# Layer 0 as 32-row products into four banks, pooling in four column groups: one change to a one-core token and attention kernel

## The reference, cut to what matters

```python
def _L0_tok_ref(x, A, W0, b0, ...):          # x: 64 x 64 frames of 75 joints and 3 channels
    x = _layer(x, A, W0, b0, g0, be0, m0, v0, relu=True)     # 3 -> 128
    x = _layer(x, A, W1, b1, g1, be1, m1, v1, relu=True)     # 128 -> 128
    x = _layer(x, A, W2, b2, g2, be2, m2, v2, relu=False)    # 128 -> 64
    return x.mean(axis=2)                                    # mean over the 75 joints
# _layer: x @ W over channels, A @ x over joints, bias, normalisation, relu
h = tok(x);  h = concat([h, txt], axis=1)                    # 64 x 96 x 64
h = h + attention(layernorm(h))
h = h + ffn(layernorm(h))                                    # 30 steps of tanh, silu, layernorm, matmul
```

## Time and profile before

| | |
|---|---|
| median of three runs | 2138.03 us |
| lowest, highest run | 2136.45, 2356.8 us |
| profiled execution, first to last instruction (span) | 2132.7 us |
| PE busy | 1903.4 us (89%) |
| DVE busy | 1674.5 us (79%) |
| ACT busy | 1153.7 us (54%) |
| `tokenise` starts / the stage after it starts | 180.8 / 1562.8 us |
| mean granted clock of TensorE | 0.977 |

### The profile page before, as it was taken

How to read it: one execution, slowest core, us unless ns; L and a number is a source line. 1 busy time by engine, 2 the same in 40 slices (tenths; PEclk the granted TensorE clock), 3 DMA queues, 4 the chain that set the end, 5 groups by cost and what they waited for, 6 DMA issues and landing times. The chain is left out here.

```text
span 2132.7 us, 61654 instructions
## 1 busy us (share of the span) xinstructions
PE 1903.4 (89%) x20166; PEld 1487.2 (70%) x20166; DVE 1674.5 (79%) x4836; ACT 1153.7 (54%) x2296; POOL 484.8 (23%) x431
## 2 busy tenths in 40 slices
PE   2316399999999999999999999999957799999998
PEld 2315277777777777777777777777747477777776
DVE  3205388888888888888888888888865788888887
ACT  0103266666666666666666666666614366666665
POOL 5000000000000000000000000000004699999997
PEclk9999699999999999999999999999987799999999
DMA  3333100000000000000000000000041100000000
GB/s 111 75 71 63 44 3 3 3 3 3 3 3 3 3 3 3 3 3 3 3 3 3 3 3 3 3 3 3 3 95 32 29 0 0 0 0 0 0 0 30
DMA packets 38153, 33.35 MB, mean 16 GB/s; under 512 B 13781, under 2 KB 35477, under 8 KB 37141
## 3 DMA queue, kind: packets, MB, share of 16 engines
q1 hardware_dynamic: 36159, 32.21, 6.4%
q10 hardware_dynamic: 1972, 0.86, 0.2%
HBM read 22.02 MB, written 11.03 MB: 15 GB/s over the span
## 5 line engine op out<-in xcount | busy, mean ns | idle before, releaser
L614 ACT ACTIVATE z1hi<-ps 128x375 f16<-128x375 f32 x820 | 398.7, 486 | 405.1 <-PE ps L556 405.1
L554 PE MATMUL ps<-AThi,y0hi 125*128 125x150 f16 x2460 | 567.1, 241 | 36.5 <-DVE z1lo L650 34.6
L555 PE MATMUL ps<-ATlo,y0hi 125*128 125x150 f16 x2460 | 584.9, 238 | 0.0
L650 DVE TENSOR_TENSOR z1lo<-ps,z1hi 128x375 f16<-128x375 f32 x820 | 445.8, 544 | 171.3 <-ACT z1hi L614 171.2
L556 PE MATMUL ps<-AThi,y0lo 125*128 125x150 f16 x2460 | 564.8, 239 | 0.0
L655 DVE TENSOR_TENSOR y<-ps,negb 125x384 f32<-125x384 f32 x820 | 451.1, 550 | 37.2 <-PE ps L571 37.2
L569 PE MATMUL ps<-W1hi,z1hi 128*128 128x128 f16 x2460 | 455.2, 219 | 0.2 <-DVE y L655 0.2
L571 PE MATMUL ps<-W1hi,z1lo 128*128 128x128 f16 x2460 | 454.1, 219 | 0.0
L570 PE MATMUL ps<-W1lo,z1hi 128*128 128x128 f16 x2460 | 453.6, 219 | 0.0
L645 DVE SCALAR_TENSOR_TENSOR y0lo<-ps,y0hi 125x512 f16<-125x512 f32 x615 | 420.7, 684 | 1.1 <-ACT y0hi L610 1.1
L610 ACT ACTIVATE y0hi<-ps 125x512 f16<-125x512 f32 x615 | 363.4, 591 | 13.4 <-PE ps L536 13.4
(11 more groups left out here) (197 smaller groups left out, 2315.4 us busy)
## 6 DMA issues: line engine op xcount, KB each, us to landing
pooled_parts<-stage SPq DMA_DIRECT2D x410, 4.0 KB
zk<-z_parts SPq DMA_DIRECT2D x16, 360.4 KB
parts<-pooled_parts SPq DMA_DIRECT2D x16, 256.0 KB, 5.7
xs<-in_x_v SPq DMA_DIRECT2D x3, 1201.2 KB
xs<-in_x_v SPq DMA_DIRECT2D x5, 720.7 KB
z_parts<-zp SPq DMA_DIRECT2D x20, 180.2 KB
pooled_parts<-stage SPq DMA_DIRECT2D x205, 2.0 KB
pooled_parts<-stage SPq DMA_DIRECT2D x205, 10.0 KB
```

What stands on the lines that cost most here:

```text
L554: nc.tensor.matmul(o, hi, ahi, start=(ph == 0), stop=False, skip_group_check=True)
L555: nc.tensor.matmul(o, hi, alo, start=False, stop=False, skip_group_check=True)
L614: nc.scalar.activation(z1hi[:, q, 0:GV], ps[:, Z1B + q % 2, 0:GV], ACT.Identity).then_inc(z1hi_done, 1)
L650: nc.vector.tensor_tensor(z1lo[:, q, 0:GV], ps[:, Z1B + q % 2, 0:GV], z1hi[:, q, 0:GV], ALU.subtract).then_inc(z1lo_done, 1)
```

## The change

Layer 0 becomes twelve products of 32 rows and 128 columns. For each piece, quarter q multiplies rows 32q to 32q + 31 of the operand with the matching rows of `W0K`, and writes to bank q (banks 0 to 3, three times 128 columns each). The operand is no longer a slice of `zk` at an address from a register, but one of two fixed buffers `z_static` (`zst`), which SP fills by a transfer (`fetch`) two iterations ahead. y0 high and low become four steps of 384 columns, one for each quarter, in place of three of 512. The twelve products stand together, after mix of quarter 1. Pooling becomes twelve float32 products of 128 columns: quarter q writes output partitions 32q to 32q + 31, the three pieces add up in PSUM, and the result lies in the last 128 columns of bank 0, beside layer 0's. `stage` is then 128 x 128, SP stores it in four transfers to one array, and the addition in `tokens` is gone.

The core of the diff:

```diff
-        y0hi = sb("y0hi", [P, 2, PH, QUART * C], F16)
-        y0lo = sb("y0lo", [P, 2, PH, QUART * C], F16)
+        ZW = GV + 3
+        zst = sb("z_static", [P, 2, ZW + 1], F16)
+        y0hi = sb("y0hi", [P, 2, QUART, PH * C], F16)
+        y0lo = sb("y0lo", [P, 2, QUART, PH * C], F16)
         z1hi = sb("z1hi", [P, QUART, PH * P], F16)
         z1lo = sb("z1lo", [P, QUART, PH * P], F16)
         y1 = sb("y1", [P, 2, QUART, PH * C])
-        stage = sb("stage", [96, 2, QUART, C])
-
+        stage = sb("stage", [P, 2, C])
...
-        STORES = [(0, 0, 2, 0), (0, 2, 1, 32 + MID), (0, 3, 2, 64 + 3), (1, 0, GF, 32)]
-        Y0B, Z1B, Y1B, PLB = 0, 3, 5, 7
+        Y0B, Z1B, Y1B = 0, 4, 6
+        PLC = PH * C
...
+        def pooled_rows(it):
+            return pooled_dram.rearrange("(q f) c -> q f c", q=QUART)[:, bass.ds(it * GF, GF)]
...
+                def fetch(it, par):
+                    sp.dma_start(zst[:, par, 0:GV], zk[:, bass.ds(it * GV, GV)]).then_inc(zst_loaded[par], 16)
+
+                def store(it, par):
+
+                    sp.wait_ge(staged, it + 1)
+                    for q in range(QUART):
+                        sp.dma_start(pooled_rows(it)[q], stage[32 * q:32 * q + GF, par]).then_inc(stored[par], 16)
+
                 for i in range(1, len(REGIONS)):
                     load_region(sp, zk, zs, i, z_loaded[1])
+                sp.wait_ge(z_loaded[0], QUART * 2 * 16)
+                sp.wait_ge(zst_clear, 1)
+                fetch(0, 0)
+                fetch(1, 1)
 
                 def body(it, par, pair, last=False):
 
-                    sp.wait_ge(staged, it + 1)
-                    for part, f0, n, row in STORES:
-                        dst = pooled_dram[part].rearrange("(q f) c -> f q c", q=QUART)[bass.ds(it * GF + f0, n)]
-                        sp.dma_start(dst, stage[row:row + n, par]).then_inc(stored[par], 16)
-                steps(sp, body)
+                    if not isinstance(it, int) or it + 2 <= LAST:
+                        sp.wait_ge(y0_ready, it + 1)
+                        fetch(it + 2, par)
+                    if late(it, 2):
+                        store(it - 2, par)
+                steps(sp, body, (NEAR, lambda: sp.wait_ge(z_loaded[1], (len(REGIONS) - 1) * QUART * 2 * 16)))
+                store(LAST - 1, 1)
+                store(LAST, 0)
...
-                def layer0(it, ph):
-
-                    n = it * PH + ph
-                    if late(n, PH):
-                        pe.wait_ge(y0lo_done, n - PH + 1)
-                    nc.tensor.matmul(ps[:, Y0B + ph, :], zk[:, bass.ds(it * GV + ph * R, P)],
-                                     W0K[:].rearrange("p q c -> p (q c)"), start=True, stop=True).then_inc(y0_ready, 1)
+                def layer0(it, par, loads):
+
+                    if late(it, 1):
+                        pe.wait_ge(y0lo_done, it * QUART)
+                    if late(it, 3):
+                        pe.wait_ge(staged, it - 2)
+                    pe.wait_ge(zst_loaded[par], loads * 16)
+                    for ph in range(PH):
+                        for q in range(QUART):
+                            rows = slice(32 * q, 32 * q + 32)
+                            last = nc.tensor.matmul(ps[:, Y0B + q, ph * C:(ph + 1) * C], zst[rows, par, ph * R:ph * R + P],
+                                                    W0K[rows, q, :], start=True, stop=True, skip_group_check=True)
+                    last.then_inc(y0_ready, 1)
 
                 def mix(it, par, q):
 
-                    if q == 0:
-                        pe.wait_ge(y0hi_done, it * PH + PH)
-                        pe.wait_ge(y0lo_done, it * PH + PH)
                     m = it * QUART + q
+                    pe.wait_ge(y0lo_done, m + 1)
                     if late(m, 2):
                         pe.wait_ge(z1lo_done, m - 1)
                     for ph in range(PH):
                         w = SPAN[ph][1] * V
                         o = ps[:, Z1B + q % 2, SPAN[ph][0] * V:SPAN[ph][0] * V + w]
-                        hi = y0hi[0:R, par, ph, q * C:(q + 1) * C]
-                        lo = y0lo[0:R, par, ph, q * C:(q + 1) * C]
+                        hi = y0hi[0:R, par, q, ph * C:(ph + 1) * C]
+                        lo = y0lo[0:R, par, q, ph * C:(ph + 1) * C]
...
-                def pool_joints(it, par):
+                def pool_joints(it, par, above):
 
                     pe.wait_ge(y1_done, it * QUART + QUART)
-                    if late(it, 1):
-                        pe.wait_ge(staged, it)
+                    pe.wait_ge(y0lo_done, above)
                     for ph in range(PH):
-                        last = nc.tensor.matmul(ps[32 * ph:32 * ph + 32, PLB, :].rearrange("p (q c) -> p q c", q=QUART),
-                                                abar[0:R, ph, :], y1[0:R, par, :, ph * C:(ph + 1) * C],
-                                                start=True, stop=True)
+                        for q in range(QUART):
+                            last = nc.tensor.matmul(ps[32 * q:32 * q + 32, Y0B, PLC:PLC + C], abar[0:R, ph, :],
+                                                    y1[0:R, par, q, ph * C:(ph + 1) * C],
+                                                    start=(ph == 0), stop=(ph == PH - 1), skip_group_check=True)
                     last.then_inc(pooled_ready, 1)
...
-                pe.wait_ge(z_loaded[0], QUART * 2 * 16)
-                for ph in range(PH):
-                    layer0(0, ph)
+                layer0(0, 0, 1)
 
                 def body(it, par, pair, last=False):
 
                     for q in range(QUART):
                         mix(it, par, q)
-                        if q < PH and not last:
-                            layer0(it + 1, q)
+                        if q == 1 and not last:
+                            layer0(it + 1, 1 - par, pair + 2)
                         if q == QUART - 1 and late(it, 1):
-                            pool_joints(it - 1, 1 - par)
+                            pool_joints(it - 1, 1 - par, it * QUART + (QUART if last else QUART + 1))
...
-                def y0_high(it, par, ph):
-                    act.wait_ge(y0_ready, it * PH + ph + 1)
-                    nc.scalar.activation(y0hi[0:R, par, ph, :], ps[0:R, Y0B + ph, :], ACT.Relu).then_inc(y0hi_done, 1)
+                def y0_high(it, par, q):
+                    act.wait_ge(y0_ready, it + 1)
+                    nc.scalar.activation(y0hi[0:R, par, q, :], ps[0:R, Y0B + q, 0:PH * C], ACT.Relu).then_inc(y0hi_done, 1)
...
-                    nc.scalar.activation(stage[:, par].rearrange("p q c -> p (q c)"), ps[0:96, PLB, :],
-                                         ACT.Identity).then_inc(staged, 1)
-
-                for ph in range(PH):
-                    y0_high(0, 0, ph)
+                        act.wait_ge(stored[par], half * (QUART * 16))
+                    nc.scalar.activation(stage[:, par], ps[:, Y0B, PLC:PLC + C], ACT.Identity).then_inc(staged, 1)
...
+                    z1_high(it, 0)
+                    y0_high(it, par, 3)
+                    z1_high(it, 1)
+                    z1_high(it, 2)
+                    if not last:
+                        y0_high(it + 1, 1 - par, 0)
+                    z1_high(it, 3)
+                    if not last:
+                        y0_high(it + 1, 1 - par, 1)
+                        y0_high(it + 1, 1 - par, 2)
...
-                def y0_low(it, par, ph):
-                    dve.wait_ge(y0hi_done, it * PH + ph + 1)
-                    nc.vector.scalar_tensor_tensor(y0lo[0:R, par, ph, :], ps[0:R, Y0B + ph, :], 0.0,
-                                                   y0hi[0:R, par, ph, :], ALU.max, ALU.subtract).then_inc(y0lo_done, 1)
+                def y0_low(it, par, q):
+                    dve.wait_ge(y0hi_done, it * QUART + q + 1)
+                    nc.vector.scalar_tensor_tensor(y0lo[0:R, par, q, :], ps[0:R, Y0B + q, 0:PH * C], 0.0,
+                                                   y0hi[0:R, par, q, :], ALU.max, ALU.subtract).then_inc(y0lo_done, 1)
...
+                    if late(it, 1):
+                        relu1(it - 1, 1 - par, 1)
+                    z1_low(it, 0)
+                    y0_low(it, par, 3)
+                    if late(it, 1):
+                        relu1(it - 1, 1 - par, 2)
+                    z1_low(it, 1)
+                    if late(it, 1):
+                        relu1(it - 1, 1 - par, 3)
+                    z1_low(it, 2)
+                    if not last:
+                        y0_low(it + 1, 1 - par, 0)
+                    relu1(it, par, 0)
+                    z1_low(it, 3)
+                    if not last:
+                        y0_low(it + 1, 1 - par, 1)
+                        y0_low(it + 1, 1 - par, 2)
...
-                def sum_parts(g):
-                    t = slice(g * TG, (g + 1) * TG)
-                    dve.wait_ge(parts_loaded[g], PARTS * 16)
```

(17 more changed lines are left out.)

38 lines of the change are left out of this document (16 added, 22 removed).

## The result

The changed kernel takes **2268.07 us** (median of 4 runs, 2265.64 to 2274.99) against 2138.52 beside it (4 runs): 1.062 times as long, 95% interval 1.060 to 1.064. I had said 2283 us and slower. One of the four runs before, 2356.8 us, fell in a slower state and isn't in the ratio. The profiled execution is the longest of the four, 2274.99 us with a span of 2272.8.

The account below looks back on a forecast made before the run. PE was taken to bound the kernel, with two new waits making the period 7.12 us. Span 2132.7 + 149.9 (later last iteration) - 5 (`tokens`) = 2277.6 us, plus 5.3 to the median: 2283 us, range 2235 to 2350.

Parts of the forecast that it names:

- The 6.11 us: PE's own work per iteration of the loop if it never waits, 0.4 us less than before the change.
- 0.82 for pooling after a wait: New pooling on PE: passes 0.65, load 0.03, stagger 0.02, switch 0.09, given as about 0.82 us; 0.90 without a wait.
- a step of 0.108: Layer 0 on PE if weight loads can't hide in the 0.055 us step: 0.108 per step, 0.57 us in all.
- the high end: Upper range limit, 2350 us, from a milder no-overlap form: one more pooling pass and layer 0 at 0.57, adding 65 us.
- The 3.07 times: Skill page's speedup for four row tiles: layer 0 at 0.22 us, the sum some 28 us lower; cited, not adopted.
- My 0.36 after a wait: Layer 0's twelve products on PE once it has been waiting, 0.36 us; 0.45 when it has not.
- a way of 1.78 us against a cover of 1.19: Mix's end through z1 low and y0 low to PE, against PE's meanwhile work: 0.59 us idle before layer 0 and pooling.
- 7.12 expected: Loop period: 3.33 us from layer 0 to pooling plus 3.79 to the next layer 0, 0.6 more than before.
- 245.3 for layer 0: Stage start: first fetch stands behind SP's 16 zk loads, so layer 0 starts at 245.3 us; 4.5 early iterations lost.
- The copies are fast enough: Rival: both waits in the loop vanish, period 6.11 us, time 2078 us, faster by 2.8%; chance 3%.
- The waits are shorter: Rival: each loop wait 0.25 to 0.45 us shorter, period 6.2 to 6.6, time 2095 to 2181 us; chance 5%.
- The tiles don't overlap: Rival: layer 0 and pooling take 0.85 + 2.7 us on PE, some 2750 us; chance 5% for the hard form.

Follow-up runs that it names:

- experiment 3: Changed kernel with layer 0 moved behind the third mix and pooling moved to the end of the iteration: 2058.72 us, ratio 0.965 to the kernel before.
- Experiments 1, 2 and 4: Changed kernel with pooling one layer-1 group later, 2171.48 us; with layer 0 one mix later, 2085.29; with y0 copies reordered on ACT and DVE, 2061.43.
- experiments 9 to 11: Far zk loads spread, one per iteration for 16 iterations: on experiment 3 1999.27 us, on the kernel before 2102.78, on the changed kernel 2208.99.
- experiment 6: Experiment 3 with layer 0 and pooling products issued tile by tile instead of pass by pass: 2209.84 us, ratio 1.035 to the kernel before.
- experiment 7: Changed kernel with SP's first two fetches issued ahead of the 16 far zk loads: 2266.03 us, ratio 1.061 to the kernel before.

## Why the prediction was right

- **PE's own work.** The 6.11 us that I worked out for a PE that never waits is 6.055 in experiment 3. Layer 0 came out at 0.38 for 0.45, pooling at 0.88 for 0.90. Tiles on different rows do run side by side: twelve products in 0.28, the first four started within 0.012 (from 800.759 on). Two figures of the prediction don't follow from their terms: 0.65 + 0.03 + 0.02 + 0.09 is 0.79 and not 0.82 for pooling after a wait (measured: 0.79), and with a step of 0.108 layer 0 would be 3 x 0.108 + 0.05 + 0.04 + 0.10 = 0.51 and not 0.57, which puts the high end some 12 us too high. Neither touches the result.
- **The rule on tiling.** The 3.07 times of the Trainium skill, page "TensorE: Matmul & The Clock Gate", section "Measured speedup vs the span model", would have made layer 0 0.22 us. Measured: 0.66 / 0.28 = 2.4 times behind a wait, 0.66 / 0.38 = 1.7 with the switch. The page's factor is for products of 512 columns; here they have 128, and that start and switch weigh more in these is my reading, which no run tests. My 0.36 after a wait counts from y0 low's landing, and so did 800.76 - 800.69 + 0.28, with y0 low ended at 800.63 and 0.06 to PE: 0.35.
- **The two waits.** Expected a way of 1.78 us against a cover of 1.19, 0.59 each. Measured 1.79 at pooling and 1.86 at layer 0, and PE stands 0.59 and 0.67. The 0.07 more at layer 0 is the part of its own start that I had put to layer 0. Experiments 1, 2 and 4 take either wait away by its cause.
- **The period.** 7.12 expected, 7.096 measured: pooling is 0.03 shorter and the chain ahead of it 0.01 longer, and layer 0 with its chain takes the 2.14 that were forecast. 203 periods gave 4.8 us less.
- **The start.** Forecast 245.3 for layer 0 and 254.1 for the second iteration's first mix; measured 250.66 and 258.34. SP's loads began 3.5 us later in this execution (184.29 for 180.81), and I had left out the fetch's own landing, 1.9 us. The way from there took 7.7 us for my 8.8. That the fetch stands behind the loads, which cost 4.5 iterations already made under them, was the right mechanism: experiments 9 to 11.
- **What comes after the loop.** The last iteration's first mix came at 1698.90 (1699.5 forecast), the way from there to the next stage is 1.35 us shorter than before (I had it the same), and `tokens` lost 4.25 us (5). The 3.6 us by which the later stages are shorter weren't in the sum. They go with the granted clock in `attention`, which isn't the same from one kernel to the next: in the three kernels with the old layer 0 the way from its first product to `feed_forward` takes 67.0 to 67.5 us, at 0.64 to 0.66 over the first 20 us; in the ten with the new one 63.1 to 65.9, at 0.90 to 0.77. Why the clock rises sooner in one than in the other stays open. The span is 4.8 under my 2277.6. To the median another 10.0 are lost: I had added 5.3 for the distance to the span, it was 2.2 in this execution, and the execution profiled lies 6.9 above the median. That the forecast of a span came within 5 us is in part luck: a start 4.2 us too late and periods 4.8 too short in sum cancel. The 7.12 is not luck, since each of its parts was found.
- **The rivals.** "The copies are fast enough" named the right threshold: it became true, at 2059 us, once the order gave the chain more than 1.78 us of cover, and not because a link was shorter. "The waits are shorter" is false: 0.59 and 0.67. "The tiles don't overlap" is false for this order; experiment 6 shows a mild form of it in another.

## What to carry to other kernels

When products are made cheaper and moved, write down for each new wait the way from the last thing it depends on and the work that the waiting engine has meanwhile: here 1.78 us against 1.19, on an engine that was the bound, ate a saving of 0.48 and 0.57 more, and moving one call by one mix gave nearly all of it back (a period of 6.17, against 6.055 with no wait left). A small transfer that the loop needs at once must not stand behind a large one that it needs later, nor run beside it; spreading the large one cost about 3 us here and gained 59 net. And packed tiles are better issued round by round than tile by tile, by 0.72 us in pooling and by 0.03 in layer 0.

## What the runs showed of the hardware

- Going from full-array products to 32-row or 32-column ones costs PE 0.08 to 0.10 us: 0.17 between the starts 800.88 and 801.05, where a product takes 0.07, and 0.14 between 802.98 and 803.12, where it takes 0.06. At pooling the type changes as well, from float16 to float32; no run parts the two.
- The order of twelve float32 products (24 records) in four column groups decides between 0.80 and 1.52 us.
- After PE's 75 us pause the column of the granted clock reads 1.00 for 250 to 260 us, and yet the first mix product lasts 0.30 us (252.35) where the same one lasts 0.24 at 258.34, and 0.31 before, where the column read 0.50. The steps between starts say it more plainly: products of 225 columns step 0.19 us here (252.89 to 253.08) and 0.10 in the loop (799.60 to 799.70). In experiment 7, after a pause of 58 us, the same products last 0.33 as well (251.87), and there the column reads 0.50 from 250 to 256 us. So they point to the lower of the two levels (1.2 and 2.4 GHz) for some 3 us that the column doesn't show; from 255.85 on the records last 0.24 again.
- In the kernels after the change and in the one before, `attention` takes 63.15 and 67.20 us for the same work, at a granted clock of 0.90 and 0.65 over its first 20 us.
- A 94 KB copy that lands in 1.9 us in the steady loop takes 32 us beside 4.3 MB of loads on another queue.
